# Softmax attention: the two score sets of a head move from free-axis halves to the two halves of the partitions

## The reference, cut to what matters

```python
qkv = x @ Wqkv                       # x: (2, 1024, 256)
q1, k1, q2, k2, v = jnp.split(qkv, [C, 2 * C, 3 * C, 4 * C], axis=-1)   # C = 128
q1, k1, q2, k2 = (heads(t, HEAD_DIM) for t in (q1, k1, q2, k2))         # 16 heads of 8
v = heads(v, 2 * HEAD_DIM)
A1 = _causal_sdpa(q1, k1, v)         # softmax(mask(q k^T / sqrt(8))) v
A2 = _causal_sdpa(q2, k2, v)
diff = A1 - lam * A2
diff = (1.0 - LAMBDA_INIT) * diff / rms(diff)
out = diff @ Wproj
```

## Time and profile before

| | |
|---|---|
| median of 3 runs | 1720.75 us (1720.3 to 1721.72) |
| the profiled execution | 1723.06 us, its span 1721.3 us |
| mean granted clock of TensorE | 0.951 of full speed |
| PE, PEld busy | 1514.0, 1018.7 us |
| DVE, ACT, POOL busy | 1265.1, 1107.9, 1094.0 us |
| first maxima unit, first score tile | 67.7, 100.6 us |
| last score tile | 592.9 us |
| exponentials, L615 | 576, 317.8 us, mean 600 ns |
| maxima, L520 | 640, 364.1 us, mean 627 ns |
| unit products, L647 | 768, 243.0 us, mean 344 ns |
| mask products, L650 | 512, 107.1 us, mean 228 ns |
| score products, L683 | 768, 220.7 us, mean 331 ns |
| value products, L703 | 1536, 154.6 us, mean 498 ns |

### The profile page before, as it was taken

The page is one execution under the profiler, slowest core; times in us unless marked ns, Lnnn a source line. Parts: engine busy times, 40 slices in busy tenths (PEclk is TensorE's granted clock), DMA queues, the critical chain, the costliest instruction groups (busy, mean ns, idle before and its releaser), DMA issues. The chain is left out here.

```text
span 1721.3 us, 26790 instructions
## 1 busy us (share of the span) xinstructions
PE 1514.0 (88%) x8532; PEld 1018.7 (59%) x8532; DVE 1265.1 (73%) x3421; ACT 1107.9 (64%) x2384; POOL 1094.0 (64%) x1285
## 2 busy tenths in 40 slices
PE   7799999999999745697838999999999999887998
PEld 4334434344343234575726788878888888776665
DVE  5688887888887036643456999999999999973433
ACT  3146767666676624304115999999999999994332
POOL 7205575665765643043243999999999999973353
PEclk9789999999999977999978999999999999999999
DMA  5301001010010041640100000000000100000000
GB/s 196 110 20 38 21 27 32 20 37 22 21 38 2 1 156 68 226 147 41 49 0 1 1 1 1 1 1 1 1 1 1 50 1 1 1 1 1 1 25 25
DMA packets 39813, 59.85 MB, mean 35 GB/s; under 512 B 9132, under 2 KB 33592, under 8 KB 38776
## 3 DMA queue, kind: packets, MB, share of 16 engines
q1 hardware_dynamic: 39672, 58.13, 10.1%
HBM read 40.93 MB, written 16.78 MB: 34 GB/s over the span
## 5 line engine op out<-in xcount | busy, mean ns | idle before, releaser
L615 ACT ACTIVATE a_PT<-a_sc 128x512 f32<-128x512 f32 x576 | 317.8, 600 | 191.2 <-PE a_sc L683 186.5
L520 DVE TENSOR_REDUCE a_mpart<-a_nat 128x1 f32<-128x512 f32 (+3 forms) x640 | 364.1, 627 | 79.2 <-PE a_nat L650 42.2
L2022 DVE BATCH_NORM_STATS2 c_stat<-c_R 128x6 f32<-128x512 f32 x576 | 380.9, 678 | 1.6 <-ACT c_R L1941 1.5
L1986 POOL TENSOR_SCALAR c_R<-big,c_negtau 128x256 f32<-128x256 f32 x264 | 300.7, 1167 | 35.6 <-DVE c_negtau L2055 29.0
L1986 POOL TENSOR_SCALAR c_R<-c_Z,c_negtau 128x256 f32<-128x256 f32 x255 | 290.4, 1166 | 15.8 <-DVE c_negtau L2088 15.7
L647 PE MATMUL a_nat<-mem 96*128 96x512 bf16 (+3 forms) x768 | 243.0, 344 | 15.7 <-PEq L80 9.6
L1858 PE MATMUL c_z<-mem,c_R 128*128 128x256 f32 x1024 | 231.5, 379 | 0.0
L683 PE MATMUL a_sc<-mem 128*128 128x512 bf16 (+3 forms) x768 | 220.7, 331 | 8.3 <-ACT a_PT L615 5.7
L487 POOL TENSOR_SCALAR_AFFINE_SELECT a_PT<-a_PT 128x512 f32<-128x512 f32 x128 | 79.0, 636 | 222.7 <-ACT a_PT L615 222.7
L1941 ACT ACTIVATE c_R<-c_Z,c_negtau 128x256 f32<-128x256 f32 x513 | 215.8, 515 | 0.4 <-DVE c_negtau L2088 0.4
L1941 ACT ACTIVATE c_R<-big,c_negtau 128x256 f32<-128x256 f32 x504 | 212.5, 515 | 3.1 <-DVE c_negtau L2055 1.6
(11 more groups left out here) (316 smaller groups left out, 2488.6 us busy)
## 6 DMA issues: line engine op xcount, KB each, us to landing
mem<-qk_parts SPq DMA_DIRECT2D x360, 32.0 KB
qk_parts<-a_parts SPq DMA_DIRECT2D x16, 384.0 KB, 2.6
made<-f_made SPq DMA_DIRECT2D x24, 256.0 KB, 2.8
mem<-made SPq DMA_DIRECT2D x3, 2048.0 KB, 7.9
X<-in_L_attn_x_dram SPq DMA_DIRECT2D x4, 512.0 KB, 6.9
mem<-in_L_ffn_wq_dram SPq DMA_DIRECT2D x1, 2048.0 KB, 14.9
ternary<-f_W_T SPq DMA_DIRECT2D x1, 2048.0 KB, 6.3
mem<-in_L_ffn_wo_dram SPq DMA_DIRECT2D x1, 2048.0 KB, 12.9
```

Of the source, the lines that this page charges most:

```text
L520: dve.tensor_reduce(mpart[:, b, j:j + cnt, i, k0 // 512], src, AX.X, ALU.max).then_inc(s_max, 1)
L615: act.activation(PT[:, n % 3, c, :], sc[:, u % 2, :], ACT.Exp, scale=SCALE0).then_inc(s_exp, 1)
L1986: pool.tensor_scalar(split(i, h) if r < NR else whole(i, h), scores_of(i)[:, h, :], threshold(i, r, h), 0.0, ALU.add, ALU.max).then_inc(s_ ...
L2022: dve.bn_stats(stat[:, r, b, :], R[:, slot(i), b, :]).then_inc(s_stat, 1)
```

## The change

QS and KS lose their set index. Set 0 lies on partitions 0 to 63 and set 1 on 64 to 127 (SIDE = 64): 48 rows of parts, then three rows for the maxima. Unused rows are not read any more (units read 48 rows, score tiles 51), so KS alone is filled, with ones, and QS is not cleared. A mask product has only 64 rows, so it becomes two, each with half of the identity and of the mask; for that, SP makes copies of both with their partition halves swapped. Units go set 1, 0, 1, 0, and a unit with two short pieces takes both from one set. Score tiles go set 0, 1, 0, 1 (SET_ORDER); ACT puts each in the slice of PT where it was.

```diff
--- before.py
+++ after.py
@@ -25,28 +25,20 @@
 H0, HD0, VD0 = 16, 8, 16
 SCALE0 = HD0 ** -0.5
 LAMBDA_INIT = 0.8 - 0.6 * float(np.exp(-0.3))
-STK = 6 * HD0
-MROW = 96
+STK, SIDE = 6 * HD0, 64
 NEG = -1.0e30
 BF16_ONES = 1.0 + 127.0 / 65536.0
 def max_units():
-    units = []
-    for j in range(2):
-        for i in range(3, TB):
-            units.append(([(j, i, 0, 512)], 1))
-        units.append(([(j, 7, 512, 512)], 1))
-        units.append(([(j, 2, 0, 384)], 1))
-        units.append(([(j, 6, 512, 384)], 1))
-    units.append(([(0, 1, 0, 256), (1, 1, 0, 256)], 2))
-    units.append(([(0, 5, 512, 256), (1, 5, 512, 256)], 2))
-    units.append(([(0, 0, 0, 128), (1, 0, 0, 128)], 2))
-    units.append(([(0, 4, 512, 128), (1, 4, 512, 128)], 2))
-    return units
+    shapes = [[(i, 0, 512)] for i in range(3, TB)] + [[(7, 512, 512)], [(2, 0, 384)], [(6, 512, 384)],
+                                                      [(1, 0, 256), (5, 512, 256)], [(0, 0, 128), (4, 512, 128)]]
+    return [(j, segs) for segs in shapes for j in (1, 0)]
+SET_ORDER = (0, 2, 1, 3)
 PROB_CHUNKS = [
     [(0, 0, 512)], [(0, 512, 512)], [(1, 128, 384), (3, 384, 128)], [(1, 512, 512)], [(2, 256, 256), (6, 768, 256)],
@@ -111,10 +103,11 @@
 def load_head(sp, K, n, buf, tokens, semaphore):
     for j in range(2):
         for side, (S, order) in enumerate(((K.QS, Q_PARTS), (K.KS, K_PARTS))):
             for k, part in enumerate(order):
-                sp.dma_start(S[k * HD0:(k + 1) * HD0, buf, j, tokens],
+                sp.dma_start(S[SIDE * j + k * HD0:SIDE * j + (k + 1) * HD0, buf, tokens],
                              K.qk_parts[2 * j + side, part, ds(HD0 * n, HD0), tokens]).then_inc(semaphore, 16)
@@ -137,8 +130,8 @@
         s_x = [sem(f"x{g}") for g in range(NG)]
         s_parts = [sem(f"parts{e}") for e in range(2)]
         (s_w, s_lam, s_ident, s_pool, s_pad, s_zero, s_st, s_mv, s_var, s_rstd, s_dve, s_xn, s_turned, s_xT, s_qk, s_v, s_hi, s_rest,
-         s_mid, s_lo, s_vc, s_lame) = (sem(n) for n in "w lam ident pool pad zero st mv var rstd dve xn turned xT qk v hi rest "
-                                       "mid lo vc lame".split())
+         s_mid, s_lo, s_vc, s_lame, s_swap) = (sem(n) for n in "w lam ident pool pad zero st mv var rstd dve xn turned xT qk v hi rest "
+                                       "mid lo vc lame swap".split())
         ctx.callback(sem.clear)
         block = ctx.enter_context(nc.Block())
         rows = lambda g: slice(g * GT, (g + 1) * GT)
@@ -154,6 +147,11 @@
                 sp.dma_start(K.lam_in[:, n, :], v.rearrange("(a n) -> a n", a=1).broadcast_to([P, HD0])).then_inc(s_lam, 16)
             sp.dma_start(K.w_proj[:], K.w_proj_in.rearrange("(c p) n -> p c n", p=P)).then_inc(K.s_w_proj, 16)
             load_ffn(sp, K, K.w_ffn)
+            sp.wait_ge(s_ident, 3)
+            for whole, swapped in ((K.ident_bf, K.ident_swap), (K.mask, K.mask_swap)):
+                for half in range(2):
+                    sp.dma_start(swapped[SIDE * half:SIDE * half + SIDE, :],
+                                 whole[SIDE * (1 - half):SIDE * (2 - half), :]).then_inc(s_swap, 16)
             for g in range(NG):
                 for j in range(4):
                     sp.wait_ge(s_lo, 4 * g + j + 1)
@@ -162,8 +160,9 @@
                 if g == 1:
                     for e in range(2):
                         sp.wait_ge(s_parts[e], 16 * 4)
-                    sp.wait_ge(s_zero, 3)
+                    sp.wait_ge(s_zero, 1)
                     load_head(sp, K, 0, 0, slice(0, T), K.s_first)
+            sp.wait_ge(s_swap, 64)
             for e in range(2):
                 sp.wait_ge(s_parts[e], 16 * 8)
@@ -199,22 +198,16 @@
             root(0)
             pool.wait_ge(s_xn, GT)
-            pool.memset(K.QS[:].bitcast(F32), 0.0).then_inc(s_zero, 1)
+            pool.memset(K.KS[:].bitcast(F32), BF16_ONES).then_inc(s_zero, 1)
             root(1)
             middle(0)
             root(2)
-            pool.wait_ge(s_xn, GT * 3)
-            pool.memset(K.KS[0:MROW].bitcast(F32), 0.0).then_inc(s_zero, 1)
-            pool.wait_ge(s_zero, 2)
             middle(1)
             root(3)
-            pool.wait_ge(s_xn, GT * 4)
-            pool.memset(K.KS[MROW:P].bitcast(F32), BF16_ONES).then_inc(s_zero, 1)
-            pool.wait_ge(s_zero, 3)
             middle(2)
             middle(3)
             pool.wait_ge(s_pad, 2)
-            pool.wait_ge(s_zero, 3)
+            pool.wait_ge(s_zero, 1)
         @block.vector
         def _(dve):
@@ -361,7 +354,7 @@
     qk_parts, VA = K.qk_parts, K.VA
-    units = [(b, n) + u for b in range(2) for n, u in enumerate(max_units())]
+    units = [(b,) + u for b in range(2) for u in max_units()]
     NU, NCH = len(units), len(PROB_CHUNKS)
     FIRST, GAP = (2 * NU) // 5, 2
     VLAG = 2
@@ -422,7 +415,8 @@
                 hold(sp, s_msp, h.count(1, 1), K.s_held)
                 for j in range(2):
                     for part in range(3):
-                        sp.dma_start(QS[MROW + part:MROW + part + 1, h.buf, j, :].rearrange("a (r q) -> a r q", q=P),
+                        row = SIDE * j + STK + part
+                        sp.dma_start(QS[row:row + 1, h.buf, :].rearrange("a (r q) -> a r q", q=P),
                                      msplit[16 * j:16 * j + 16, part, :]).then_inc(s_mld, 16)
             def period(h):
@@ -510,14 +504,16 @@
             dve.wait_ge(s_mdve, 1)
             def unit_maxima(h, u):
-                b, _, segs, cnt = units[u]
+                b, j, segs = units[u]
                 dve.wait_ge(s_nat, h.count(NU, u + 1))
                 if u == 0 and (not isinstance(h.n, int) or h.n > 0):
                     dve.wait_ge(s_negm, h.count(1))
-                j, i, k0, w = segs[0]
+                (i, k0, w), cnt = segs[0], len(segs)
                 src = nat[:, (NU * h.k + u) % 3, 0:cnt * w].rearrange("p (a w) -> p a w", a=cnt)
-                dve.tensor_reduce(mpart[:, b, j:j + cnt, i, k0 // 512], src, AX.X, ALU.max).then_inc(s_max, 1)
+                at = 2 * i + k0 // 512
+                dst = mpart[:, b, j].rearrange("p i k -> p (i k)")[:, at:at + 1 + (cnt - 1) * 9:9]
+                dve.tensor_reduce(dst, src, AX.X, ALU.max).then_inc(s_max, 1)
             def together(h):
                 dve.wait_ge(s_max, h.count(NU, NU))
@@ -612,7 +608,7 @@
                     for c in range(4):
                         u = 4 * n + c
                         act.wait_ge(s_sc, h.count(4 * NCH, u + 1))
-                        act.activation(PT[:, n % 3, c, :], sc[:, u % 2, :], ACT.Exp, scale=SCALE0).then_inc(s_exp, 1)
+                        act.activation(PT[:, n % 3, SET_ORDER[c], :], sc[:, u % 2, :], ACT.Exp, scale=SCALE0).then_inc(s_exp, 1)
                     if n == NCH - 3:
                         act.wait_ge(s_wb, h.count(1, 1))
                         act.activation(A[:, h.buf], Wb[:, h.buf], ACT.Abs).then_inc(s_abs, 1)
@@ -639,15 +635,17 @@
                 if not isinstance(h.n, int) or NU * h.n + u > 2:
                     pe.wait_ge(s_max, h.count(NU, u - 2))
-                b, _, segs, cnt = units[u]
-                for s, (j, i, k0, w) in enumerate(segs):
-                    out = nat[:, (NU * h.k + u) % 3, s * w:(s + 1) * w]
+                b, j, segs = units[u]
+                side, rows = slice(SIDE * j, SIDE * j + SIDE), slice(SIDE * j, SIDE * j + STK)
+                for n, (i, k0, w) in enumerate(segs):
+                    out = nat[:, (NU * h.k + u) % 3, n * w:(n + 1) * w]
                     q = b * T + i * P
                     diag = i * P - k0
-                    ins = pe.matmul(out, QS[0:MROW, h.buf, j, q:q + P], KS[0:MROW, h.buf, j, b * T + k0:b * T + k0 + w],
+                    ins = pe.matmul(out, QS[rows, h.buf, q:q + P], KS[rows, h.buf, b * T + k0:b * T + k0 + w],
                                     start=True, stop=diag >= w)
                     if diag < w:
-                        ins = pe.matmul(out[:, diag:diag + P], K.ident_bf[:], K.mask[:], start=False, stop=True)
+                        for half, (unit, mask) in enumerate(((K.ident_bf, K.mask), (K.ident_swap, K.mask_swap))):
+                            ins = pe.matmul(out[:, diag:diag + P], unit[side, :], mask[side, :], start=False, stop=half == 1)
                 ins.then_inc(s_nat, 1)
             def turn_max(h):
@@ -675,13 +673,14 @@
             def scores(h, n, c):
                 u = 4 * n + c
-                j, b = c // 2, c % 2
+                j, b = SET_ORDER[c] // 2, SET_ORDER[c] % 2
+                rows = slice(SIDE * j, SIDE * j + STK + 3)
                 if not isinstance(h.n, int) or 4 * NCH * h.n + u > 1:
                     pe.wait_ge(s_exp, h.count(4 * NCH, u - 1))
                 col = 0
                 for kt, q0, w in PROB_CHUNKS[n]:
-                    ins = pe.matmul(sc[:, u % 2, col:col + w], KS[:, h.buf, j, b * T + kt * P:b * T + (kt + 1) * P],
```

(8 more changed lines are left out.)

## The result

The changed kernel takes 1735.51 us (median of 6 runs, 1728.66 to 1742.41) against 1720.89 us (6 runs, 1720.3 to 1722.9): ratio 1.0082, 95% interval 1.0056 to 1.0107. It is slower by 0.8%, where 1718 was forecast. One of the 102 executions of the kernel before, in a later session, took 2013.2 us at a mean granted clock of 0.735 and is in no ratio here. The profiled execution is the slowest of the six, 1742.41 us around a span of 1740.6; its mean granted clock is 0.926 (before 0.951), that of the other five 0.930 to 0.936. So the profile shows the effect at its largest, 19.3 us of span where the medians differ by 14.6.

A forecast was written before the change was run, and what follows sets the result against it. PE and ACT wait for each other over two score banks, with DVE setting the time in part of each head. From 1720.75 us: -1.4 for the heads, -1.9 for clears, +0.4 for early masks, giving 1718 us; range 1698 to 1738.

The forecast's parts named there:

- I5: Interval between value products over slots 2 to 5 of a head: 3.11 us to become 3.00, -0.11.
- I6: Interval between value products over slots 6 to 9 of a head: 4.07 us, held by the copy of sums, unchanged.
- I9 to I2: Three intervals between value products, slots 18 to 29 of a head: DVE's chain sets their 10.40 us, -0.06.
- I4: Interval between value products over slots 34, 35, 0 and 1: 3.45 us to become 3.23, -0.22.
- I3: Interval between value products over slots 30 to 33: 3.10 us, +0.12 as the last score tile waits for a masked unit.
- I7: Interval between value products over slots 10 to 13: 3.64 us, +0.12 from a masked unit behind the last score tile.
- I8: Interval between value products over slots 14 to 17: 3.34 us, +0.06 with two masked units behind the score tile.
- A: Rival, slower: nothing runs side by side, so extra masks are on PE's path; 1.1 us more a head, 1735 us, chance 0.12.
- B: Rival, faster: chunk tails vanish in both halves of the head; 1.1 us less a head, 1702 us, chance 0.16.
- C: Rival, faster by far: PE stops mattering in the head loop and DVE sets all; 1638 us, chance 0.02.
- D: Rival, slower: weight loads no longer hidden when products of one half follow each other; 1737 us, chance 0.10.
- rival E: Slower: PE's granted clock falls, priced for all of the loop at some 1870 us, chance 0.05.

The follow-up runs named there:

- b_order: Kernel before with its own layout, but the changed kernel's order of units and score tiles: 1721.96 us, ratio 0.9999.
- tail_s: Changed kernel plus unread 128-row products in heads 0 to 13, from the units' end on, and five more at head 0's start: 1727.87 us, ratio 1.0040.
- b_full: Kernel before with all products starting at row 0, none side by side, units over 48 rows, score products over 128: 1828.87 us, ratio 1.0643.

## Why the prediction was wrong, point by point

**The walk through a head was right.** Score tile and unit start 0.01 us apart where the sets differ and 0.23 where they don't. Of the intervals, I5 (3.00), I6 (4.06) and I9 to I2 (10.29 against 10.34) came as forecast; I4 gained 0.12 instead of 0.22, I3 lost 0.06 instead of 0.12, I7 lost 0.16 (0.12 forecast) and I8 nothing (0.06). The sum is -0.13 to -0.14 us a head; -0.09 was forecast, within the ±0.3 that I held it at. About half of it, 0.07, comes with the order alone (b_order), which the walk had not set apart. By this term alone the kernel would be 2 us faster.

**Rivals A to D fell.** A (nothing side by side) put a head at 31.11 + 1.1 = 32.2 us; with the overlap taken away it measured 32.34, so its price was right and its condition wrong; that its 1735 us is also what the changed kernel took is luck. B would have needed tails that vanish in both halves; in slots 9 to 17 a unit still starts 0.22 to 0.23 us behind its score tile. C would have asked ACT's chain to loosen. The Trainium skill's up to 2x (TensorEngine Tiling (Array Packing), Theoretical Speedup) holds for a pair of neighbours, 0.01 us apart where it was 0.22, and is worth 1.36 us in 32.34 here, because the chunk's time is in the value products and ACT's chain, and the masks take most of that back. D (weight loads exposed) is refuted by masks that still come 0.06 us apart: I4 and I5 got shorter.

**The step that failed is rival E's reasoning.** I gave the clock 0.05 on one argument: it "stayed 1.00 in the last head at 15.24 of 20, so less PE work did not bring it down there". So the sum has no term for the clock. That argument measured PE work by its busy time. The last head before had score products over 128 rows; the change takes 128 to 51 and 96 to 48 under the same busy rows. In the same last head it fell to 0.50, and with spare products from the end of the units on, over 64 rows or over 128, it stayed at 1.00. "If the clock leaves 1.00" stood among my own signs of being wrong, and came true. My price for E, 1870 us, was for a loop wholly at half clock; it was partial: 7.1 us in three heads, 4.3 at the start, 13.9 in the last head of the profiled execution, which is 7 us longer than the median.

**The start was mis-sized.** -1.9 us was forecast for the clears, the first unit came 4.7 sooner. I counted only SP's wait of 7.2 us and left POOL's own chain as it was. But POOL's root and middle parts stand behind the clears, and every group of tokens waits for them. SP's and DVE's timeline in the changed kernel, to be read against the earlier trace rows:

```profile
38.21 8.09 SPq L110 DMA_DIRECT2D mem<-qk_parts  x24
46.34 11.26 SPq L158 DMA_DIRECT2D qk_parts<-a_parts  x8
```

```profile
56.52 0.69 DVE L239 TENSOR_TENSOR a_parts<-a_rest,a_parts 128x512 bf16<-128x512 f32 x1 [0.51 <-POOL a_parts L197]
```

DVE's last part ended at 57.21 instead of 58.38 us, and SP was through at 57.60, where I had 59.4; from there to the first unit it took 5.4 us instead of 6.4. The +0.4 for doubled masks ahead of the loop is inside the rest: first unit to first turning took 24.2 us instead of 23.6.

**What the profile was to show.** The first unit at 65.8 (63.0 measured) and ACT's wait near 186 us (203.5, from the half clock of PE) missed; the range, 1698 to 1738 us, held the median of 1735.51 by way of A and D, for a reason that neither names. The sign was wrong.

## What to carry to other kernels

When a change narrows the contraction of TensorE's products, busy time was here no measure of what it does to the granted clock: ask what becomes of the rows in use, look in the profile for the stretches with the least work on PE beside them (the last pass of a loop, the start, slots where another engine leads), and price those at half clock. Packing two sets in the halves pays only where the pairs that can overlap are on the path; here ACT's chain, the value products and the doubled masks left 0.14 us of 31, and half of that came with the order. When work leaves an engine, follow that engine's own queue and not only the one wait that named it.

## What the runs showed of the hardware that I had not expected

- With PE busy for 300 of 300 us (299.87 with 51 rows), the granted clock averaged 1.00, 0.84 and 0.55 with score products over 128, 72 and 51 rows. In the last head the changed kernel's 51-row score products and value products ran at 0.50 with PE busy 38.76 of 46 us, and at 1.00 with spare products beside them from the end of the units on, of 64 rows by 512 columns or 128 by 256.
- A switch between a product over 128 rows and one over 48 costs 0.10 us each way (0.32 instead of 0.22).
- Products on different halves start 0.01 us apart with their weight loads, and loads on one half are hidden as well: masks 0.06 us apart.
- The low stretches in the loop met other heads in each kernel, but began at one place of a head, some 5 us after the turning of the maxima. The times of the changed kernel scatter more (1728.66 to 1742.41 us against 1720.3 to 1722.9 before). What starts a low stretch in one head and not in another was not settled.
- Nor was the rise at the start: it is later in tail_s than without its extra products, and in b_full, with score products over 128 rows and units over 48, it comes at 116 to 120 us, as late as in the changed kernel.
